# A gated delta rule on one core: the state of the recurrence in SBUF in place of PSUM

## The chip, the cores and the metric

The kernel runs on one core of a Trainium2 chip. The metric is the device time of one execution in microseconds; the median of three runs before the change is 888.05 us (886.9 to 889.43).

## The reference, cut to what matters

Two layers work on x of 16 x 512 x 128 (batch, tokens, width), in float32. The change touches the first layer's recurrence alone:

```python
# layer 0, attention: 16 heads of width 8; k = q = rmsnorm(x_act per head)
def step(S, inp):                     # S: [B, H, 8, 8], one matrix per batch and head
    q_t, k_t, v_t = inp
    S = S * lam
    err = v_t - jnp.einsum('bhk,bhkv->bhv', k_t, S)
    S = S + beta * (k_t[..., :, None] * err[..., None, :])
    o_t = jnp.einsum('bhk,bhkv->bhv', q_t, S)
    return (S, o_t)
_, o = jax.lax.scan(step, S0, (qT, kT, vT))        # 512 steps, one after the other

# layer 0, feed forward, beside it
h = silu(x @ w1.T * s1) * (x @ w2.T * s2)          # 128 -> 512
h = gelu(h @ h1.T * t1); h = gelu(h @ h2.T * t2)   # 512 -> 512, twice
y = h @ w3.T * s3                                  # 512 -> 128
```

A second layer with linear attention and a low-rank feed forward follows.

## The kernel before

The kernel has three stages, each with one instruction stream per engine: `prepare` (to about 179 us) makes keys, factors and right-hand sides for every batch; `recur_and_feed_forward` (about 179 to 617 us) runs the recurrence and the feed forward of the first layer side by side; `second_layer` does the rest.

In the second stage the recurrence lies on VectorE alone. The 256 pairs of batch and head are laid over 128 partitions in G = 2 groups. Four tokens are solved at once as a block (BLK = 4), so the 512 tokens are 128 blocks, one after the other. Each block is five VectorE instructions, each waiting for the one before:

- L910: the state (128 numbers a partition) times the four tokens' rows `tok_p`, written to `pg` (512 products a partition);
- L916: a sum over the 8 products and one more slot that ScalarE has filled with the right-hand side, written to `w`;
- L919: `w` times the block's keys `blk_k`, written to `kw` (512 a partition);
- L924: a sum over the four tokens, written to `gain` (128 a partition);
- L929: the new state, `lam4` x state + `gain`, in one SCALAR_TENSOR_TENSOR with a per-partition scalar.

Four blocks are a phase (PH = 4), 32 phases in all. Two PSUM banks `rec[0]` and `rec[1]` alternate by phase. Each holds `w` of a phase in its first 256 columns and, before the change, the state in the next 128. `pg`, `tok_p`, `blk_k`, `kw` and `gain` are in SBUF. The trace calls what lies in these banks `r_rec`.

The feed forward of the 16 batches runs on the other engines. TensorE multiplies (L1133 to L1140; L1165 to L1170 for the output). ScalarE applies the activations and splits each operand into an upper part (L1048, L1053). GpSimd (POOL) multiplies the two gates (`gate`, L943) and subtracts the upper parts to get the lower ones (`rest`, L935), for `f_gl`, `f_hl` and `f_xl`; it lays the tokens and keys of a segment too (L958, L966). All of POOL's operands in this stage are in SBUF. POOL's order is written out in its `batch`.

The two halves are tied in three places. ScalarE's `serve(n, i)` stands at four points of every batch and, where a phase is due, waits for `s_ok` (the state after the phase's last block), saves `w` (`save_w`, L1014) and fills the right-hand sides of the phase after next (`lay_r`, L1003). VectorE waits for `w_saved` before the last L929 of a phase, and for `r_laid` before the first L916. After the last phase ScalarE saves `w`, SyncE stores it (L846), and only when these stores have landed does the block of the stage end and `second_layer` begin.

Of the kernel before, what the change touches and what calls it, by code (L numbers as in the profile page):

```python
# [12 lines left out]
H, DH = 16, 8  # L13
HID = 512
P = 128
# [17 lines left out]
def build(nc, io, out):  # L33

    scr = {}
    for name in ("xnT", "P", "K", "R", "fac", "W"):
        scr[name] = nc.dram_tensor("scratch_" + name, [B, P, L], F32).ap()
    scr["xf"] = nc.dram_tensor("scratch_xf", [B, L, D], F32).ap()
    with ExitStack() as ctx:
        c = constants(nc, ctx)  # L40
        prepare(nc, io, scr, c)
        recur_and_feed_forward(nc, io, scr, c)
        second_layer(nc, io, scr, c, out)
# [703 lines left out]
def recur_and_feed_forward(nc, io, scr, c):  # L747
# [11 lines left out]
    TPH = PH * BLK  # L759
    SEGPH = BSEG // PH  # L760
    NPH = NSEG * SEGPH
    VG = DH * G
# [3 lines left out]
    with ctx:  # L766
        def sb(name, shape, dt=F32):
            return ctx.enter_context(nc.sbuf_tensor(name, shape, dt))
# [4 lines left out]
        def bank(name, shape):  # L773
            return ctx.enter_context(nc.psum_tensor(name, shape, F32))
# [10 lines left out]

        rec = [bank(f"r_rec{q}", [P, L]) for q in range(2)]
        w_of = [r[:, 0:VG * TPH].rearrange("p (a t) -> p a t", t=TPH) for r in rec]
        state = [r[:, VG * TPH:VG * TPH + VG * DH] for r in rec]

        x_f = c.first_x  # L790
        x_h, x_l = sb("f_xh", [P, L], F32R), sb("f_xl", [P, L], F32R)
# [866 lines left out]
```

## Time and profile before

| | before |
|---|---|
| median of 3 runs | 888.05 us |
| profiled execution, its own time | 888.89 us |
| its span, first to last instruction | 887.2 us |
| busy TensorE / VectorE / ScalarE / POOL, share of the span | 85% / 84% / 66% / 69% |
| mean granted TensorE clock | 0.943 |

A row of the trace gives the line in the kernel, the engine, the operation, the tiles written and read, their shapes and how often; then times. DVE is VectorE, ACT is ScalarE, PE is TensorE, SPq is SyncE's queue. What stands behind "<-" in brackets is what an idle engine had waited for, as the profile infers it.

### The profile page before, as it was taken

The numbers are of one execution on the slowest core, as the hardware profiler recorded it, in microseconds if no ns is written. First come the engines' busy times: TensorE is split into PE (matmuls) and PEld (weight loads), VectorE is DVE, ScalarE is ACT, GpSimd is POOL, SyncE is SP. The second block draws the span as 40 slices with busy tenths as digits, with TensorE's granted clock in tenths as the row PEclk, the third lists the DMA queues.
The fourth block names the chain that finished last, engine by engine and source line by source line (L and its number), as shares of the span: only waits on it lengthen the run. The fifth ranks groups of instructions, "written<-read, shape, count | busy, mean of one in ns | idle before, by whom it ended". The sixth has DMA issues, their size and how long they took to land. (4 is left out here: it accounts for less than half of the span.)

```text
span 887.2 us, 12736 instructions
## 1 busy us (share of the span) xinstructions
PE 751.5 (85%) x3422; PEld 531.0 (60%) x3422; DVE 747.8 (84%) x1424; ACT 584.7 (66%) x1319; POOL 608.2 (69%) x556
## 2 busy tenths in 40 slices
PE   1678888368999999999999999970389999999997
PEld 1444343146777778877777778860246666666664
DVE  2677888789999999999899898997268899989885
ACT  3666788267868777787787877720566667666631
POOL 1356888568776678686877666700298898989872
PEclk9998999759999999999999999995589999999998
DMA  6245665440511515125061160110411313222000
GB/s 172 75 164 171 222 226 206 170 96 1 106 37 35 131 35 113 53 57 109 0 130 35 35 130 24 48 36 24 143 37 48 96 52 93 61 84 84 24 25 25
DMA packets 135200, 75.68 MB, mean 85 GB/s; under 512 B 73962, under 2 KB 117612, under 8 KB 135148
## 3 DMA queue, kind: packets, MB, share of 16 engines
q1 hardware_dynamic: 132892, 72.22, 29.0%
q10 hardware_dynamic: 2256, 2.88, 1.0%
q8 instruction: 18, 0.29, 0.2%
q14 instruction: 34, 0.28, 0.1%
HBM read 41.53 MB, written 33.55 MB: 85 GB/s over the span
## 5 line engine op out<-in xcount | busy, mean ns | idle before, releaser
L935 POOL TENSOR_TENSOR f_hl<-f_h,f_hh 128x512 fp32r<-128x512 f32 x64 | 82.5, 1293 | 88.4 <-ACT f_hh L1053 88.3
L1347 POOL TENSOR_TENSOR l_kv<-l_qkv 128x1024 f32<-128x1024 f32 x64 | 124.8, 1950 | 24.7 <-PE l_ps_s L1568 21.7
L1133 PE MATMUL f_ps<-f_gh,w_hi 128*128 128x512 f32 x256 | 104.5, 408 | 6.8 <-POOL f_gl L935 6.8
L916 DVE TENSOR_REDUCE r_rec<-r_pg 128x64 f32<-128x576 f32 x128 | 97.4, 761 | 7.2
L1133 PE MATMUL f_ps<-f_hh,w_hi 128*128 128x512 f32 x256 | 102.5, 400 | 0.4 <-ACT f_b L1042 0.4
L1486 DVE TENSOR_TENSOR l_qs<-l_ps_s,l_qd 128x1024 f32<-128x1024 f32 x64 | 78.3, 1224 | 23.0 <-issue 11.2
L910 DVE TENSOR_TENSOR r_pg<-r_rec,r_pt 128x512 f32<-128x512 f32 x128 | 88.6, 692 | 6.3 <-POOL r_pt L958 1.1
L943 POOL TENSOR_TENSOR f_g<-f_a,f_b 128x512 f32<-128x512 f32 x64 | 81.6, 1286 | 16.3 <-ACT f_b L1042 16.3
L919 DVE TENSOR_TENSOR r_kw<-r_rec,r_kb 128x512 f32<-128x512 f32 x128 | 88.5, 691 | 4.4
L924 DVE TENSOR_REDUCE r_gain<-r_kw 128x128 f32<-128x512 f32 x128 | 87.8, 686 | 4.4
L935 POOL TENSOR_TENSOR f_gl<-f_g,f_gh 128x512 fp32r<-128x512 f32 x64 | 82.0, 1292 | 3.2 <-ACT f_gh L1048 3.2
L1492 DVE TENSOR_REDUCE l_o_in<-l_qs 128x128 f32<-128x1024 f32 x64 | 77.5, 1211 | 0.6
L1135 PE MATMUL f_ps<-f_gl,w_hi 128*128 128x512 f32 x192 | 77.6, 404 | 0.0
L1135 PE MATMUL f_ps<-f_hl,w_hi 128*128 128x512 f32 x192 | 75.7, 394 | 0.0
L1048 ACT ACTIVATE f_gh<-f_g 128x512 fp32r<-128x512 f32 x64 | 41.1, 642 | 52.1 <-POOL f_g L943 51.6
L1133 PE MATMUL f_ps<-f_xh,w_hi 128*128 128x512 f32 x128 | 54.9, 429 | 22.4 <-ACT f_a L1038 13.6
L1567 PE MATMUL l_ps_s<-l_kv,tri 128*128 128x512 f32 x128 | 66.9, 604 | 2.9 <-DVE l_qs L1486 2.9
L1170 PE MATMUL f_ps<-w,f_e 128*128 128x128 f32 x512 | 67.6, 275 | 0.0
L1568 PE MATMUL l_ps_s<-l_kv,tri 128*128 128x512 f32 x128 | 65.4, 593 | 0.0
L1052 ACT ACTIVATE f_h<-f_ps,t 128x512 f32<-128x512 f32 x64 | 44.5, 695 | 31.0 <-PE f_ps L1140 30.8
L1417 ACT ACTIVATE l_qkv<-l_ps_q 128x384 f32<-128x384 f32 x64 | 31.3, 490 | 48.7 <-PE l_ps_q L1554 47.3
L1133 PEld LDWEIGHTS f_ps<-f_gh,w_hi 128*128 128x128 f32 x256 | 49.6, 194 | 22.2 <-POOL f_gl L935 8.2
(202 smaller groups left out, 1997.7 us busy)
## 6 DMA issues: line engine op xcount, KB each, us to landing
p_x<-in_L_attn_x_dram SPq DMA_DIRECT2D x16, 256.0 KB, 3.3
scratch_xnT<-p_xnT SPq DMA_DIRECT2D x16, 256.0 KB, 3.3
scratch_K<-p_kout SPq DMA_DIRECT2D x16, 256.0 KB, 3.4
scratch_fac<-p_fac SPq DMA_DIRECT2D x16, 256.0 KB, 3.5
scratch_R<-p_rr SPq DMA_DIRECT2D x16, 256.0 KB, 2.4
scratch_P<-p_pp SPq DMA_DIRECT2D x16, 256.0 KB, 2.0
first_x<-scratch_xnT SPq DMA_DIRECT2D x16, 256.0 KB, 2.8
first_xt<-in_L_attn_x_dram SPq DMA_DIRECT2D x16, 256.0 KB, 3.0
```

What stands on the lines that cost most here:

```text
L910: dve.tensor_tensor(pg[q][:, at, :, :, 0:DH].rearrange("p (v g) i k -> p v g i k", g=G), by_head(state[q]), of_tokens(tok_p[u], t), ALU.mu ...
L916: dve.tensor_reduce(w, pg[q][:, at, :, :, :], AX.X, ALU.add).then_inc(w_ok, 1)
L919: dve.tensor_tensor(kw[:, :, :].rearrange("p (v g k) i -> p v g k i", v=DH, g=G), w.rearrange("p (v g) i -> p v g i", g=G).unsqueeze(3).to ...
L924: dve.tensor_reduce(gain[:, :], kw[:, :, :], AX.X, ALU.add).then_inc(gain_ok, 1)
L935: pool.tensor_tensor(lower, full, upper.bitcast(F32), ALU.subtract).then_inc(done, 1)
L943: pool.tensor_tensor(g_f[:, j, :], a_f[:, j, :], b_f[:, j, :], ALU.mult).then_inc(gate_ok, 1)
L1133: nc.tensor.matmul(bank, c.w_hi[:, weights[k], :], upper[k], start=k == 0, stop=False)
L1135: nc.tensor.matmul(bank, c.w_hi[:, weights[k], :], lower[k], start=False, stop=False)
L1170: ins = nc.tensor.matmul(y_at[:, tokens], e_f[:, k, tokens], c.w3[:, k, :], start=False, stop=t == NT - 1 and k == NB - 1)
L1347: pool.tensor_tensor(dst, k, v, ALU.mult).then_inc(kv_ok, 1)
L1486: dve.tensor_tensor(qs[t % 2][:, :].rearrange("p (h v k) -> p h v k", h=H, k=DH), ps_s[:, :, :].rearrange("p a (h v k) -> p (a h) v k", h= ...
L1492: dve.tensor_reduce(out=o_in[n % 2][:, t, :].rearrange("p (h v) -> p h v", h=H), in_=qs[t % 2][:, :].rearrange("p (h v k) -> p h v k", h=H ...
```

## The change

The state gets two SBUF tensors of its own, of 128 numbers a partition each. Nothing else is edited: `w` stays in the two PSUM banks, and the five instructions, their order and their waits are the same. `state[q]` is read by L910 and L929 and written by L894 (the first zeros) and L929.

```diff
         rec = [bank(f"r_rec{q}", [P, L]) for q in range(2)]
         w_of = [r[:, 0:VG * TPH].rearrange("p (a t) -> p a t", t=TPH) for r in rec]
-        state = [r[:, VG * TPH:VG * TPH + VG * DH] for r in rec]
+        state = [sb(f"r_state{q}", [P, VG * DH])[:, :] for q in range(2)]
```

## Rows read from the trace of the kernel before

**Rows 1.** Busy time by window, the recurrence's stretch and its tail: window, length, engines, clock, DMA.
```profile
179.00:616.80 437.80, 391.43 (x1936) 317.51 (x1936) 408.20 (x640) 316.82 (x511) 291.25 (x236) 0.96 0.26 61
...
578.00:616.80 38.80, 14.94 (x96) 12.96 (x95) 36.55 (x58) 6.24 (x12) 0.50 (x1) 0.77 0.07 21
```

**Rows 2.** Timeline, end of the stage, ScalarE, SyncE, TensorE: start, length, instruction, idle before.
```profile
616.74 0.38 ACT L1014 ACTIVATE r_w<-r_rec 128x256 f32<-128x256 f32 x1 [13.15 <-DVE r_rec L929]
...
617.15 1.25 SPq L846 DMA_DIRECT2D scratch_W<-r_w  x2
...
592.71 1.06 PE L1170 MATMUL f_ps<-w,f_e 128*128 128x128 f32 x8
```

**Rows 3.** The lines that touch the state: duration ns min/median/max, first and last start.
```profile
L910 DVE TENSOR_TENSOR r_pg<-r_rec,r_pt x128: 690/692/694, 179.0 to 613.4; 128x512 f32<-128x512 f32 x128
...
L929 DVE SCALAR_TENSOR_TENSOR r_rec<-r_rec,lam,r_gain x128: 358/359/360, 182.1 to 616.3; 128x128 f32<-128x128 f32 x128
```

**Rows 4.** Timeline of VectorE over one block.
```profile
402.57 0.36 DVE L929 SCALAR_TENSOR_TENSOR r_rec<-r_rec,lam,r_gain 128x128 f32<-128x128 f32 x1
402.97 0.69 DVE L910 TENSOR_TENSOR r_pg<-r_rec,r_pt 128x512 f32<-128x512 f32 x1
...
405.94 0.36 DVE L929 SCALAR_TENSOR_TENSOR r_rec<-r_rec,lam,r_gain 128x128 f32<-128x128 f32 x1
```

**Rows 5.** VectorE groups that differ in where operands lie: busy us, mean ns or min/median/max.
```profile
L541 DVE SCALAR_TENSOR_TENSOR p_prod<-p_ps_k,cfac,p_kT 128x128 f32<-128x128 f32 x16 | 5.5, 342 | 0.0
...
L1498 DVE TENSOR_TENSOR l_past<-l_ps_kv,head_ones x48: 278/280/294, 649.0 to 875.7; 128x128 f32<-128x128 f32 x48
...
L1510 DVE TENSOR_TENSOR biases<-biases x1: 264/264/264, 623.5 to 623.5; 128x128 f32<-128x128 f32 x1
...
L531 DVE TENSOR_TENSOR p_keys<-p_xn,p_rrms x16: 678/692/1174, 24.8 to 155.6; 128x512 f32<-128x512 f32 x16
```

**Rows 6.** A short VectorE operation of two SBUF inputs, and POOL beside it.
```profile
L1460 DVE TENSOR_TENSOR l_nm<-l_mean,l_rs x16: 163/678/682, 634.4 to 840.5; 128x4 f32<-128x4 f32 x16
...
653.59 0.66 DVE L1460 TENSOR_TENSOR l_nm<-l_mean,l_rs 128x4 f32<-128x4 f32 x1
...
652.28 1.95 POOL L1347 TENSOR_TENSOR l_kv<-l_qkv 128x1024 f32<-128x1024 f32 x1 [0.79 <-PE l_ps_s L1568]
```

**Rows 7.** Timeline of VectorE and POOL around L531, the longest and one other.
```profile
155.64 1.17 DVE L531 TENSOR_TENSOR p_keys<-p_xn,p_rrms 128x512 f32<-128x512 f32 x1
...
155.23 1.04 POOL L346 TENSOR_TENSOR p_kout<-p_kT,kfac 128x512 f32<-128x512 f32 x1
...
111.05 0.68 DVE L531 TENSOR_TENSOR p_keys<-p_xn,p_rrms 128x512 f32<-128x512 f32 x1
...
111.42 1.16 POOL L256 TENSOR_TENSOR p_tmp_p<-p_coup,p_pp 128x384 f32<-128x384 f32 x1 [0.32 <-ACT p_coup L439]
...
37.40 1.00 POOL L256 TENSOR_TENSOR p_tmp_p<-p_coup,p_pp 128x384 f32<-128x384 f32 x1 [6.78 <-ACT p_coup L439]
```

**Rows 8.** POOL's costliest groups in the recurrence's stretch: busy us, mean ns, idle before.
```profile
L935 POOL TENSOR_TENSOR f_hl<-f_h,f_hh 128x512 fp32r<-128x512 f32 x64 | 82.5, 1293 | 88.4 <-ACT f_hh L1053 88.3
L935 POOL TENSOR_TENSOR f_gl<-f_g,f_gh 128x512 fp32r<-128x512 f32 x64 | 82.0, 1292 | 3.2 <-ACT f_gh L1048 3.2
L943 POOL TENSOR_TENSOR f_g<-f_a,f_b 128x512 f32<-128x512 f32 x64 | 81.6, 1286 | 16.3 <-ACT f_b L1042 16.3
```

**Rows 9.** Timeline of POOL: two operations back to back, and one spaced by ScalarE.
```profile
414.44 2.55 POOL L935 TENSOR_TENSOR f_gl<-f_g,f_gh 128x512 fp32r<-128x512 f32 x2
...
424.82 1.29 POOL L935 TENSOR_TENSOR f_hl<-f_h,f_hh 128x512 fp32r<-128x512 f32 x1 [0.59 <-ACT f_hh L1053]
```

**Rows 10.** TensorE after an idle stretch, twice, and the window behind the first.
```profile
218.78 0.50 PE L1133 MATMUL f_ps<-f_gh,w_hi 128*128 128x512 f32 x1 [1.74 <-POOL f_gl L935]
...
219.80:223.20 3.40, 3.18 (x8) 2.56 (x9) 3.14 (x6) 3.39 (x8) 1.41 (x2) 0.50 0.27 67
...
256.54 0.50 PE L1133 MATMUL f_ps<-f_xh,w_hi 128*128 128x512 f32 x1 [1.44 <-ACT f_a L1038]
```

## The prediction, made before the changed kernel was run

> **What bounds the kernel now.** I read the busy time by window first, because the change lies in one stage. From 179.0 to 616.8 us VectorE runs 640 instructions, the 128 blocks of five, and is busy 408.20 of 437.80 us; TensorE is busy 391.43 us, POOL 291.25 us with 236 operations [rows 1]. Both TensorE and VectorE look like the bound there. The end of the stage decides. The timeline of ScalarE shows it idle for 13.15 us before its last save of `w`, for L929, and SyncE's store of `w` follows at 617.15 us [rows 2]; from 578 us on POOL has one operation (of 236) and VectorE is busy 36.55 of 38.80 us [rows 1]. So the feed forward is over well before the recurrence, and the second layer waits for the recurrence. TensorE's last matmuls of the stage end at 593.8 us [rows 2]: the feed forward has 23 us of room. Every nanosecond added to each block is 128 ns on the end.
>
> Next the blocks. L910 takes 690 to 694 ns and L929 358 to 360 ns over all 128 [rows 3]. Nothing disturbs them, though POOL is at work two thirds of the time. One block lasts 405.94 - 402.57 = 3.37 us from L929 to L929; L910 starts 0.04 us after the end of L929 (402.93 to 402.97), and from the end of L910 (403.66) to the next L929 are 2.28 us, filled by L916, L919 and L924 [rows 4].
>
> **What is removed and added, 1: the operations themselves.** No instruction comes or goes. L910 gets its first input from SBUF in place of PSUM; its nearest row of the same shape with both inputs in SBUF, L531, has the median 692 ns, the same as L910 now [rows 3, 5]: nothing gained. L929 gets its state from SBUF and writes it there. The nearest rows: the same operation with a PSUM input but an SBUF output and a per-partition scalar, L541, 342 ns against 359 ns; and TENSOR_TENSOR of 128 columns with one PSUM input, 280 ns (L1498), against 264 ns with none (L1510) [rows 3, 5]. So L929 gains 17 ns for its output and 0 to 16 ns for its input. I take 17 ns, since the reading of the input shows 0 in L910's pair: 128 x 0.017 = 2.2 us gained, at most 128 x 0.033 = 4.2 us. The zeroing of the state (L894) is one instruction and moves by nothing that counts.
>
> The Trainium skill would price this part otherwise. Its page "VectorE: DVE Perf Modes", in the table under "The TRN2 errata", gives VectorE a fixed 58 cycles from SBUF against 120 from PSUM at 0.96 GHz. By it each of the 256 instructions would gain 62 cycles, 65 ns, together an estimated 16.5 us. The pairs of rows above show 0 and 16 ns for it.
>
> **2: what the two instructions now have in common with POOL.** After the change L910 reads two SBUF inputs (state and `tok_p`), and L929 too (state and `gain`). Before it each had one in PSUM. The trace has operations of that kind beside POOL. L1460 (two SBUF inputs, 4 columns) takes 163 ns at its shortest but 678 ns as the median of 16 [rows 6]. At 653.59 us it starts while POOL's L1347 runs (652.28 to 654.23) and ends at 654.25: it takes its 0.16 us only as POOL ends [rows 6]. The remainder of POOL's operation was 0.64 us and the delay 0.66 - 0.16 = 0.50 us, so the delay is the remainder less 0.14. L531 shows the same at 155.64 us: 1.174 us in place of 0.692, a delay of 0.48 us against a remainder of 0.63 us [rows 5, 7]. It goes the other way too: POOL's L256 starts at 111.42 us in L531 and takes 1.16 us, where it takes 1.00 us alone; the remainder of L531 was 0.31 us [rows 7]. So the two exclude each other, whoever is there first keeps the other out, and the second starts about 0.14 us before the first's recorded end.
>
> The Trainium skill, "SBUF — State Buffer", "Who interferes with whom", has this as a rule: a VectorE instruction with two SBUF inputs contends with a GpSimd instruction that reads SBUF for a shared port, and the first holds it for its whole length. It speaks against this change, and by it alone, with holds of the whole 1.29 us, the same working as below would give an estimated 0.39 us in place of 0.31 for each operation, 978 us in place of 959. Rows 6 and 7 bear out who waits, but show the hold 0.14 us shorter, and I go by them.
>
> **The price.** POOL has 236 operations in the stretch [rows 1], of which 192 take 82.5 + 82.0 + 81.6 us, 1.28 to 1.29 us each [rows 8], and the other 44 the rest, some 1.0 us each; I price all as the 192, which asks at most 4 us too much. Take one of 1.29 us that comes at a random time of a block of 3.36 us.
> - If it is running when L929 starts, L929 waits 0 to 1.29 - 0.14 = 1.15 us, 0.57 us in the mean. The chance is 1.15 / 3.36 = 0.34, the share 0.195 us.
> - If it comes in the 0.36 us of L929 or the 0.04 us behind it, it runs before L910 gets its turn. L910 then waits from 0.97 us (POOL held back until 0.14 us before L929's end: 1.29 - 0.14 - 0.04 = 1.11 left, less 0.14) to 1.15 us (POOL just begun), about 1.0 us. The chance is 0.40 / 3.36 = 0.12, the share 0.12 us.
> - If it comes in L910 it waits itself, at most 0.55 us, and then runs under L916 and L919, which read `w` or `pg` and have at most one SBUF input that matters: no delay.
>
> Together 0.31 us for each operation of POOL, 236 x 0.31 = 73 us.
>
> A second reading of the same trace, without chance: of the 128 starts of L929, 74 fall into a running operation of POOL, and the remainders less 0.14 us sum to 40.0 us; 29 operations of POOL start in L929 or within 0.40 us of its start, at about 1.0 us each 29 us. That is 69 us (the 128 starts run from 182.1 to 616.3 us [rows 3], POOL's 236 operations stand in the same window [rows 1]).
>
> A third for the densest stretches, where POOL starts every 1.25 us [rows 9]: after L910 two of its operations fit into 2.28 us plus 0.14 and L929 is hardly late; the third comes in L929, and L910 waits 0.97 us for it. That is about 0.95 us for three operations, 0.32 us each. Where POOL is spaced by 1.86 us [rows 9] against blocks of 3.36 us there is no fixed relation, and the first sum holds.
>
> I take 73 us. Less 2.2 us it is 71 us on the recurrence, whose stretch becomes 437.8 + 71 = 509 us.
>
> **What stands beside it.** The feed forward is held up too: operations of POOL that come in L910 or L929 wait up to 0.55 or 0.22 us. 40 of them start in L910 and 29 in or near L929; at 0.28 and 0.1 us that is 14 us if all lay on its path, less than its 23 us of room and far less than 23 + 71. So it costs nothing. It will rather be held back: ScalarE waits at `serve` once a phase, some 71 / 32 = 2 us each. TensorE then idles. After an idle stretch of 1.74 us the granted clock fell from 1.0 to 0.50 (the lower of TensorE's two levels, 1.2 GHz against 2.4) for 3.4 us, and after one of 1.44 us matmuls kept 0.50 us and less, the pace of the full clock [rows 10]. A fall per phase would cost 1.7 us of TensorE's work each, 32 x 1.7 = 54 us, under the 94 us of room that it then has. Costed at nothing, too. Nothing in stages one and three reads the state.
>
> **The sum** against the profiled execution: 888.89 + 73 - 2.2 = 959.7 us. The median of the runs was 0.84 us lower, so I forecast 959 us.
>
> **The rivals.**
> - *No contention* (faster). The recurrence's two instructions would be left alone because their records now are, and only their operands' place counts: 2.2 to 4.2 us gained, 884 to 886 us; by the skill's table 872 us, worked out above. For it: L541 and L1498, 48 times within 278 to 294 ns [rows 5], are undisturbed beside POOL. Against it: both have a PSUM input, and L1460 was held in 14 of 16. It decides if a two-input instruction with a broadcast input doesn't take part; L531 has one and was held. 0.05 for faster; 0.03 that the gain and a handful of collisions cancel.
> - *POOL yields* (slower by little). If VectorE always came first, POOL would pay: 128 x (0.55 + 0.22) = 99 us of its time is closed, two thirds of it in use, some 65 us; beyond the 23 us of room the feed forward would end the stage 42 us later, 928 us. Against it: rows 6 show VectorE as the one that waits. 0.04.
> - *POOL first at every hand-over* (slower). In the dense stretches a third operation of POOL takes its turn before L929, and a fourth before L910: 1.24 + 0.97 us for four operations, 0.56 us each. For all 236 that is 132 us, 1018 us. It asks that the next operation's request counts from the end of the one before, though it starts behind L929's. 0.07.
> - *The clock* (slower). If TensorE falls to 1.2 GHz for 10 us rather than 3.4 at every pause, it loses 5 us a phase, 160 us in all, and the feed forward sets the end: 888.9 - 23 + 160 = up to 1025 us. Against it: such a feed forward would leave no pauses, and the clock would stay up; the two meet near 975 to 990 us. 0.08.
>
> **How the numbers follow.** The forecast case has 0.73, with its own range 930 to 990: the price per operation between 0.19 us (only L929's share counts: 236 x 0.195 - 2 = 44 us, 932 us) and 0.44 us (half-way to POOL first: 104 - 2 = 102 us, 990 us). Outside lie the faster and same cases (0.08), part of POOL first and of the clock; I reach up to 1000 for the clock and down to 926 for POOL yields. The range is 926 to 1000 us. Faster by over 0.3% 0.05, within 0.3% 0.03, slower by over 0.3% 0.92; 0.3% is about what a measurement of this kernel can tell from no change.
>
> **What would show each step.** Durations of L910 and L929 now constant would spread: L910's median near 692 ns with a tail to about 1.8 us, L929's minimum 340 to 345 ns with a tail to 1.5 us; their sum would grow by some 71 us, while L916, L919 and L924 keep their 2.28 us from the end of L910 to the start of L929 [rows 4]. Each long one ends 0.02 to 0.1 us from the end of a POOL operation. The stretch of the recurrence ends near 688 us, ScalarE waits for L929 once a phase, TensorE's share of the stage falls from 0.89 to 0.77, and the second layer is unchanged. The prediction is wrong if L910 and L929 stay constant, or if ScalarE no longer waits for L929 at the end.

## The result and the profile after

The changed kernel takes 973.07 us as the median of four runs, the kernel before 888.24 us in the same comparison: 1.0953 times as long, with a 95% interval of 1.0928 to 1.0978. The forecast was 959 us, with 926 to 1000 us as its range. The profiled execution took 974.93 us with a span of 973.2 us, 86.0 us more than the span before.

The first view is part 5 of the page of the changed kernel, the five lines of the recurrence (line, engine, operation, shapes and count, then busy us, mean ns, and idle us before them):

```profile
L910 DVE TENSOR_TENSOR r_pg<-r_state,r_pt 128x512 f32<-128x512 f32 x128 | 143.2, 1119 | 6.2 <-POOL r_pt L958 1.1
...
L916 DVE TENSOR_REDUCE r_rec<-r_pg 128x64 f32<-128x576 f32 x128 | 97.4, 761 | 7.2
L919 DVE TENSOR_TENSOR r_kw<-r_rec,r_kb 128x512 f32<-128x512 f32 x128 | 88.5, 691 | 4.5
L924 DVE TENSOR_REDUCE r_gain<-r_kw 128x128 f32<-128x512 f32 x128 | 87.8, 686 | 4.4
...
L929 DVE SCALAR_TENSOR_TENSOR r_state<-r_state,lam,r_gain 128x128 f32<-128x128 f32 x128 | 81.0, 632 | 4.6
```

L910 has grown from 88.6 us (128 x 692 ns, [rows 3]) to 143.2 us and L929 from 46.0 us to 81.0 us. The other three keep their mean lengths of the trace before (761, 691 and 686 ns). The idle time before L929 was 8.3 us in the same part of the page before and is 4.6 us now. 54.6 + 35.0 - 3.7 = 85.9 us: that is the whole difference.

The same two lines in the view of single lines (ns min/median/max) answer to [rows 3], where both were flat:

```profile
L910 DVE TENSOR_TENSOR r_pg<-r_state,r_pt x128: 691/694/1805, 179.0 to 699.4; 128x512 f32<-128x512 f32 x128
...
L929 DVE SCALAR_TENSOR_TENSOR r_state<-r_state,lam,r_gain x128: 350/352/1510, 182.1 to 702.4; 128x128 f32<-128x128 f32 x128
```

More than half of the instances are undisturbed, the others are up to 1.16 us longer. Counted over all 128: 58 of L910 are longer by 54.8 us in all over their undisturbed length, 53 of L929 by 35.9 us. The timeline shows against what. First VectorE, then POOL, in a dense stretch of gate products:

```profile
423.30 1.47 DVE L929 SCALAR_TENSOR_TENSOR r_state<-r_state,lam,r_gain 128x128 f32<-128x128 f32 x1
424.80 1.64 DVE L910 TENSOR_TENSOR r_pg<-r_state,r_pt 128x512 f32<-128x512 f32 x1
...
428.72 0.35 DVE L929 SCALAR_TENSOR_TENSOR r_state<-r_state,lam,r_gain 128x128 f32<-128x128 f32 x1
429.10 1.67 DVE L910 TENSOR_TENSOR r_pg<-r_state,r_pt 128x512 f32<-128x512 f32 x1
...
433.05 0.35 DVE L929 SCALAR_TENSOR_TENSOR r_state<-r_state,lam,r_gain 128x128 f32<-128x128 f32 x1
```

```profile
423.34 1.27 POOL L935 TENSOR_TENSOR f_gl<-f_g,f_gh 128x512 fp32r<-128x512 f32 x1
424.57 1.31 POOL L943 TENSOR_TENSOR f_g<-f_a,f_b 128x512 f32<-128x512 f32 x1
425.85 2.99 POOL L935 TENSOR_TENSOR f_gl<-f_g,f_gh 128x512 fp32r<-128x512 f32 x2
428.81 1.41 POOL L935 TENSOR_TENSOR f_xl<-first_x,f_xh 128x512 fp32r<-128x512 f32 x1
```

L929 starts at 423.30 and POOL's L935 0.04 us later, and yet L929 is the one that waits: it ends at 424.77, so its own 0.35 us began at 424.42, 0.19 us before POOL's recorded end (424.61). POOL's next operation has started at 424.57, inside L929, and now L910 waits for it: it ends at 426.44, so its 0.69 us began at 425.75, 0.13 us before that operation's end (425.88). The two POOL operations from 425.85 take 2.99 us in place of some 2.55, because the first came in L910 and is held back itself. At 428.72 L929 is free, since POOL comes 0.09 us behind it, and L910 is held. This last block, 428.72 to 433.05, lasts 4.33 us, the one before it 5.42.

It is the same for all 111 held instances: the work of the 53 of L929 begins 0.20 to 0.21 us before the end of a POOL operation that reads SBUF, that of the 58 of L910 0.13 to 0.15 us. Near ties at L929 mostly go to POOL: in 11 of the 53 the POOL operation started after L929, by up to 0.08 us, and only twice did L929 stay free of an operation that came as close behind it. At L910 there was no such tie to see.

The end of the stage, SyncE, ScalarE and TensorE, answers to [rows 2]:

```profile
702.74 0.38 ACT L1014 ACTIVATE r_w<-r_rec 128x256 f32<-128x256 f32 x1 [13.13 <-DVE r_state L929]
703.14 1.25 SPq L846 DMA_DIRECT2D scratch_W<-r_w  x2
...
669.83 1.06 PE L1170 MATMUL f_ps<-w,f_e 128*128 128x128 f32 x8
```

The recurrence still sets the end, 86.0 us later than before, and the feed forward ends 31.8 us ahead of it.

### The profile page after: what moved, and what is told of

It is laid out like the page before. It is cut to its first block and busy times, and to the rows that moved or that the text cites. A ratio compares the mean times of both kernels' runs of the same rounds, so it can differ in the third digit from the quotient of the medians.

```text
span 973.2 us, 12736 instructions
## 1 busy us (share of the span) xinstructions
PE 783.4 (81%) x3422; PEld 550.8 (57%) x3422; DVE 838.0 (86%) x1424; ACT 582.7 (60%) x1319; POOL 635.9 (65%) x556
## 5 line engine op out<-in xcount | busy, mean ns | idle before, releaser
L935 POOL TENSOR_TENSOR f_hl<-f_h,f_hh 128x512 fp32r<-128x512 f32 x64 | 87.0, 1379 | 114.0 <-ACT f_hh L1053 113.9
L910 DVE TENSOR_TENSOR r_pg<-r_state,r_pt 128x512 f32<-128x512 f32 x128 | 143.2, 1119 | 6.2 <-POOL r_pt L958 1.1
L1133 PE MATMUL f_ps<-f_xh,w_hi 128*128 128x512 f32 x128 | 63.5, 496 | 58.0 <-ACT f_a L1038 37.1
L943 POOL TENSOR_TENSOR f_g<-f_a,f_b 128x512 f32<-128x512 f32 x64 | 89.1, 1401 | 31.9 <-ACT f_b L1042 31.9
L916 DVE TENSOR_REDUCE r_rec<-r_pg 128x64 f32<-128x576 f32 x128 | 97.4, 761 | 7.2
L935 POOL TENSOR_TENSOR f_gl<-f_g,f_gh 128x512 fp32r<-128x512 f32 x64 | 90.7, 1427 | 11.4 <-ACT f_gh L1048 11.4
L919 DVE TENSOR_TENSOR r_kw<-r_rec,r_kb 128x512 f32<-128x512 f32 x128 | 88.5, 691 | 4.5
L924 DVE TENSOR_REDUCE r_gain<-r_kw 128x128 f32<-128x512 f32 x128 | 87.8, 686 | 4.4
L1014 ACT ACTIVATE r_w<-r_rec 128x256 f32<-128x256 f32 x32 | 12.4, 386 | 128.6 <-DVE r_state L929 128.6
L929 DVE SCALAR_TENSOR_TENSOR r_state<-r_state,lam,r_gain 128x128 f32<-128x128 f32 x128 | 81.0, 632 | 4.6
L1170 PE MATMUL f_ps<-w,f_e 128*128 128x128 f32 x512 | 75.4, 296 | 0.0
L1133 PEld LDWEIGHTS f_ps<-f_xh,w_hi 128*128 128x128 f32 x128 | 28.0, 219 | 79.6 <-ACT f_a L1038 44.3
L1170 PEld LDWEIGHTS f_ps<-w,f_e 128*128 128x128 f32 x512 | 70.8, 214 | 0.0
L1567 PE MATMUL l_ps_s<-l_kv,tri 128*128 128x512 f32 x128 | 66.9, 604 | 2.9 <-DVE l_qs L1486 2.9
```

The source lines that it names most:

```text
L910: dve.tensor_tensor(pg[q][:, at, :, :, 0:DH].rearrange("p (v g) i k -> p v g i k", g=G), by_head(state[q]), of_tokens(tok_p[u], t), ALU.mu ...
L916: dve.tensor_reduce(w, pg[q][:, at, :, :, :], AX.X, ALU.add).then_inc(w_ok, 1)
L919: dve.tensor_tensor(kw[:, :, :].rearrange("p (v g k) i -> p v g k i", v=DH, g=G), w.rearrange("p (v g) i -> p v g i", g=G).unsqueeze(3).to ...
L924: dve.tensor_reduce(gain[:, :], kw[:, :, :], AX.X, ALU.add).then_inc(gain_ok, 1)
L935: pool.tensor_tensor(lower, full, upper.bitcast(F32), ALU.subtract).then_inc(done, 1)
L943: pool.tensor_tensor(g_f[:, j, :], a_f[:, j, :], b_f[:, j, :], ALU.mult).then_inc(gate_ok, 1)
```

## The experiments

All are edits of the changed kernel but for the second. The comparisons stand against runs of the kernel before on the same chip, whose medians were 889.7 to 890.2 us. "Excess" is the sum, over the 128 instances in the profiled execution, of what each took beyond its undisturbed length, and a held instance is one that took over 40 ns more.

**The gain in PSUM, so that L910 alone has two SBUF inputs.**

```diff
-        gain = sb("r_gain", [P, VG * DH])
...
+        gain_at = [r[:, VG * TPH:VG * TPH + VG * DH] for r in rec]
...
-                            dve.tensor_reduce(gain[:, :], kw[:, :, :], AX.X, ALU.add).then_inc(gain_ok, 1)
+                            dve.tensor_reduce(gain_at[q], kw[:, :, :], AX.X, ALU.add).then_inc(gain_ok, 1)
...
-                            dve.scalar_tensor_tensor(out=state[after], in0=state[q], scalar=c.lam4[:, :], in1=gain[:, :],
+                            dve.scalar_tensor_tensor(out=state[after], in0=state[q], scalar=c.lam4[:, :], in1=gain_at[q],
```

> The state stays in SBUF and the block's gain goes to the PSUM columns that the state has left, so L929 has one SBUF input (state) and one PSUM input (gain), and L910 alone still has two SBUF inputs. Theory (two SBUF inputs exclude POOL): L929 is constant near 350 to 360 ns as before, L910 alone is held, in some 60 to 75 of 128 blocks and by about 0.6 us in the mean (it now meets POOL operations at a random point), 236 x 0.195 = 46 us, so the time is about 932 us (920 to 945). Rival (an instruction that reads the state from SBUF is slowed by POOL's traffic whatever its other input is): L929 is still stretched by some 36 us, and the time stays near 973 us.

It took 937.74 us, 1.0525 times the kernel before (1.0498 to 1.0552). The view of single lines:

```profile
L910 DVE TENSOR_TENSOR r_pg<-r_state,r_pt x128: 691/1067/1816, 181.3 to 665.2; 128x512 f32<-128x512 f32 x128
...
L929 DVE SCALAR_TENSOR_TENSOR r_state<-r_state,lam,r_rec x128: 346/348/350, 184.4 to 668.1; 128x128 f32<-128x128 f32 x128
```

L929 reads the same state from the same SBUF tensor beside the same POOL operations and is flat in all 128; what differs is that its second input is in PSUM. So it is not the reading of SBUF that is held but the pair. L910 is held 77 times, excess 53.5 us, where I expected 46.

The trace shows where the 7 us more come from: POOL's operations are no random arrivals here either. VectorE, then POOL, in a stretch of gate products:

```profile
409.90 1.52 DVE L910 TENSOR_TENSOR r_pg<-r_state,r_pt 128x512 f32<-128x512 f32 x1
...
414.09 1.53 DVE L910 TENSOR_TENSOR r_pg<-r_state,r_pt 128x512 f32<-128x512 f32 x1
```

```profile
410.83 1.73 POOL L943 TENSOR_TENSOR f_g<-f_a,f_b 128x512 f32<-128x512 f32 x1
412.53 2.54 POOL L935 TENSOR_TENSOR f_gl<-f_g,f_gh 128x512 fp32r<-128x512 f32 x2
```

POOL's operation of 410.83 us comes in the first L910, waits, and runs as L910 ends. The two behind it follow without a gap, and the second of them is still running (to 415.07) when the next L910 starts at 414.09: it is 0.84 us longer. Of the 77 holds 34 are of 0.74 to 0.86 us and make 27.6 of the 53.5 us; spread evenly over 0 to 1.15 us, some 8 of the 77 would lie there.

**L929 alone with two SBUF inputs.** The kernel before, state in PSUM, with a constant tensor of zeros in the state's place in L929, so the old state is left out of the update.

```diff
+        still = sb("r_still", [P, VG * DH])
...
+                dve.memset(still[:, :], 0.0)
...
-                            dve.scalar_tensor_tensor(out=state[after], in0=state[q], scalar=c.lam4[:, :], in1=gain[:, :],
+                            dve.scalar_tensor_tensor(out=state[after], in0=still[:, :], scalar=c.lam4[:, :], in1=gain[:, :],
```

> The kernel before (state in PSUM), but L929 takes its first input from a constant SBUF tensor of zeros in place of the state, so the old state is left out of the update; its output goes to PSUM. L929 has two SBUF inputs, L910 has not. Theory: L910 stays at 692 ns in all blocks, L929 is held in about 74 blocks and by 40 to 46 us in all, time about 931 us (920 to 942). Together with the run with the gain in PSUM the two parts then sum to about the whole 85 us, if held L929 and held L910 don't make each other likelier; if a held L929 draws the next POOL operation in front of L910 (43 of 53 times in the changed kernel), each part alone is a different mixture: L910 hits that follow a held L929 are missing here. Rival (the SBUF read or write of the state is what costs, not the pair): L929 undisturbed, 888 us.

It took 923.73 us, 1.0363 times (1.0334 to 1.0393). The lines (L912 and L931 are L910 and L929 here):

```profile
L912 DVE TENSOR_TENSOR r_pg<-r_rec,r_pt x128: 691/691/695, 180.1 to 648.5; 128x512 f32<-128x512 f32 x128
...
L931 DVE SCALAR_TENSOR_TENSOR r_rec<-r_still,lam,r_gain x128: 359/719/1477, 183.2 to 651.5; 128x128 f32<-128x128 f32 x128
```

The other way round: L910 is flat, L929 held 76 times with an excess of 38.2 us. The count of the trace before had said 74 times and 40.0 us. Both parts alone sum to 53.5 + 38.2 = 91.7 us, the change to 54.8 + 35.9 = 90.7 us. That the sums agree doesn't show that the two add up: in the changed kernel most of L910's excess stands behind a held L929 (below), and where L910 is held alone there is none.

**POOL writes but does not read.** In the 208 gate products and lower parts:

```diff
-                    pool.tensor_tensor(lower, full, upper.bitcast(F32), ALU.subtract).then_inc(done, 1)
+                    pool.memset(lower.bitcast(F32), 0.0).then_inc(done, 1)
...
-                    pool.tensor_tensor(g_f[:, j, :], a_f[:, j, :], b_f[:, j, :], ALU.mult).then_inc(gate_ok, 1)
+                    pool.memset(g_f[:, j, :], 0.0).then_inc(gate_ok, 1)
```

> The changed kernel, but POOL's gate products and lower parts (L935, L943, 208 operations) are memsets of the same tiles: they write SBUF and read none, and the feed forward's values are left out. The 28 copies of tokens and keys stay. Theory (only operations of POOL that read SBUF and VectorE's with two SBUF inputs exclude each other): L910 and L929 are held by the 28 copies alone, 28 x 0.385 = 11 us, the recurrence's stretch is about 445 us and the time about 895 us (886 to 905). Rival (writes count as well): memsets hold it too, in proportion to their length; at 0.5 us and more each that is some 20 to 40 us more, 915 us or above.

It took 893.29 us, 1.0035 times (1.0021 to 1.0048). The excess is 9.1 us, 5 instances of L929 and 7 of L910, and each of the 12 lies over one of the 28 copies. Of the instances that are not held 89 overlap a memset by more than 0.1 us. The timeline shows both, VectorE and POOL:

```profile
201.88 1.12 DVE L929 SCALAR_TENSOR_TENSOR r_state<-r_state,lam,r_gain 128x128 f32<-128x128 f32 x1
203.04 1.46 DVE L910 TENSOR_TENSOR r_pg<-r_state,r_pt 128x512 f32<-128x512 f32 x1
...
201.78 2.17 POOL L966 COPY r_kb<-r_k 128x512 f32<-128x512 f32 x2
...
407.95 0.69 DVE L910 TENSOR_TENSOR r_pg<-r_state,r_pt 128x512 f32<-128x512 f32 x1
...
407.82 0.53 POOL L943 MEMSET f_g<- 128x512 f32 x1
```

The copies (201.78 to 203.95) hold L929 and then L910; the memset (407.82 to 408.35) runs through L910's first half and it takes its 0.69 us. So POOL's reads are what excludes, and its writes don't. The Trainium skill, "SBUF — State Buffer", "Who interferes with whom", says just this of two SBUF inputs against a GpSimd instruction that only writes, and the run agrees: 0 of 89 held.

**The same bytes in twice as many instructions.** Each gate product and each lower part is cut into two of 256 columns:

```diff
-                    pool.tensor_tensor(lower, full, upper.bitcast(F32), ALU.subtract).then_inc(done, 1)
+                    for half in (slice(0, L // 2), slice(L // 2, L)):
+                        ins = pool.tensor_tensor(lower[:, half], full[:, half], upper[:, half].bitcast(F32), ALU.subtract)
+                    ins.then_inc(done, 1)
... (the same for the gate products)
```

> The changed kernel, with each gate product and each lower part of POOL cut into two instructions of 256 columns, the same bytes in twice as many instructions of an estimated 0.73 us. Theory (who comes first keeps the other out for its whole instruction): a wait is at most as long as one instruction, so L910 and L929 are held more often but for less: (0.59 x 0.59 / 2 + 0.40 x 0.43) / 3.36 = 0.10 us for each of 416, with the copies about 52 us, with follow-ups some 60 us; time about 945 us (930 to 957), longest L910 about 1.3 us in place of 1.8. Rival (the two share a bandwidth, and what costs is POOL's traffic): nothing changes but POOL's own length, 973 us or slower.

It took 944.48 us, 1.0609 times (1.0581 to 1.0638):

```profile
L910 DVE TENSOR_TENSOR r_pg<-r_state,r_pt x128: 691/1101/1460, 179.2 to 668.0; 128x512 f32<-128x512 f32 x128
...
L929 DVE SCALAR_TENSOR_TENSOR r_state<-r_state,lam,r_gain x128: 352/532/1224, 182.3 to 671.0; 128x128 f32<-128x128 f32 x128
```

More are held (81 and 88), each for less (longest L910 1.46 us in place of 1.81), excess 59.6 us. A shared bandwidth would have left it at 90.7 us, since the bytes are the same and POOL is busier (361.6 us in the recurrence's stretch against 318.9). The wait is for one instruction, and shorter instructions make shorter waits.

**w in SBUF too**, a third instruction of the block with two SBUF inputs:

```diff
-        w_of = [r[:, 0:VG * TPH].rearrange("p (a t) -> p a t", t=TPH) for r in rec]
+        w_of = [sb(f"r_solved{q}", [P, VG * TPH])[:, :].rearrange("p (a t) -> p a t", t=TPH) for q in range(2)]
```

> The changed kernel with w in SBUF as well, so that no tensor of the recurrence is in PSUM. L919 (w times keys) then has two SBUF inputs too, a third instruction of the block. Theory: L919 is held where POOL runs at its start, another 0.195 us for each of 236 operations less what no longer falls on L929, +25 to +46 us on the changed kernel: about 1008 us (995 to 1022). Rival (POOL's operations are bound to meet L910 or L929 in any case, so a third meeting point adds nothing): 973 us.

It took 986.13 us, 1.1067 times (1.1015 to 1.1119), 13 us more than the changed kernel: between the two expectations, nearer to the rival's.

```profile
L910 DVE TENSOR_TENSOR r_pg<-r_state,r_pt x128: 691/1448/1777, 183.6 to 714.6; 128x512 f32<-128x512 f32 x128
...
L919 DVE TENSOR_TENSOR r_kw<-r_solved,r_kb x128: 691/792/1832, 185.3 to 716.1; 128x512 f32<-128x512 f32 x128
...
L929 DVE SCALAR_TENSOR_TENSOR r_state<-r_state,lam,r_gain x128: 351/526/1278, 186.8 to 717.6; 128x128 f32<-128x128 f32 x128
```

L919, flat everywhere else, is now held 69 times, which confirms the rule for a third line. But its excess is 16.5 us, L929's has fallen from 35.9 to 18.5 us and L910's has risen from 54.8 to 67.8: in all 102.8 us against 90.7 (this profiled execution, of 990.09 us, was the longest of its four). My price per line and operation, 0.195 us, does not add up over more lines. That a meeting with POOL is mostly moved from one line to another, and seldom added, is how I read it; no run shows it by itself.

**What doubled L910's share.** In the changed kernel a held L929 is followed by a held L910 in 43 of 53 cases, and only 15 of L910's 58 stand alone. The 43 make 39.9 us of L910's excess, the 15 make 14.7 us. The trace shows why this can be: POOL's next operation is queued right behind the one that held L929 (424.57 above) and comes in L929. If so, anything that keeps POOL's next reading operation away for 0.25 us should free L910. Here a useless write stands behind each gate product and each lower part:

```diff
+        filler = sb("f_filler", [P, 384])
...
+                def fill():
+                    if fills:
+                        pool.wait_ge(filled, len(fills))
+                    fills.append(pool.memset(filler[:, :], 0.0).then_inc(filled, 1))
...
                     pool.tensor_tensor(lower, full, upper.bitcast(F32), ALU.subtract).then_inc(done, 1)
+                    fill()
... (and behind the gate products)
```

> The changed kernel, and behind each gate product and each lower part POOL writes zeros to a tile of 384 columns that nobody reads (a memset, some 0.4 us, no SBUF input). POOL's next reading operation then starts 0.4 us or more after the one before it has ended, later than the 0.25 us after which a held L929 is followed by L910. Theory (L910's excess is twice what I had forecast because POOL's next operation, queued right behind the one that held L929, comes in L929 and runs before L910): blocks in which both are held fall from 43 to under 10, L929's excess stays at 30 to 40 us, L910's falls from 54.7 to 20 to 30 us, time 945 to 955 us, though POOL has 208 instructions more. Rival (L910 is held as often as it is because POOL is busy, whatever stands before): L910's excess stays at 50 us or more, and the time at 973 us or above.

It took 934.08 us, 1.0504 times (1.0477 to 1.053): 39 us less than the changed kernel, with 208 more instructions on POOL. The lines (L912 and L931 are L910 and L929 here), and, from the groups by line, what POOL adds:

```profile
L912 DVE TENSOR_TENSOR r_pg<-r_state,r_pt x128: 691/692/1658, 181.9 to 660.2; 128x512 f32<-128x512 f32 x128
...
L931 DVE SCALAR_TENSOR_TENSOR r_state<-r_state,lam,r_gain x128: 351/604/1426, 185.0 to 663.2; 128x128 f32<-128x128 f32 x128
...
L941 POOL MEMSET f_filler<- 128x384 f32 x208 | 86.7, 417 | 0.0
```

Held L929 that are followed by a held L910 fall from 43 to 6, L910's excess from 54.8 to 8.2 us. L929's stays at 35.5 us, though spread over 103 instances in place of 53. So the follow-up is shown: it goes when POOL's next read comes later. Less is left than I had expected (8.2 in place of 20 to 30 us), and that is not the follow-up alone, which made 39.9 of the 54.8 us: of the 15 held L910 that stood alone 4 are left too. The writes set the distance of all of POOL's reads, behind a held L929 or not, and this run doesn't part the two effects.

**Fewer reading operations.** Only the 64 lower parts of the hidden layers become memsets, so they are left out of the products:

```diff
-                    rest(h_f[:, o, :], h_h[:, o, :], h_l[:, o, :], hl_ok)
+                    pool.memset(h_l[:, o, :].bitcast(F32), 0.0).then_inc(hl_ok, 1)
```

> The changed kernel with only the 64 lower parts of the hidden layers (f_hl) replaced by memsets, so that 172 reading operations of POOL remain in the stretch, and those lower parts are left out of the products. Theory (a price for each reading operation): the excess of L910 and L929 together is between the 9.1 us of 28 operations and the 90.7 us of 236, near 172 x 0.385 = 66 us; the time about 949 us (940 to 957). Rival (the dense runs of the gates cost it, and the spaced f_hl little): the excess stays above 80 us, the time above 962 us.

It took 955.55 us, 1.0735 times (1.071 to 1.076), with an excess of 69.9 us (29.5 on L929, 40.4 on L910). With 28, 172 and 236 reading operations the excess is 9.1, 69.9 and 90.7 us, 0.33, 0.41 and 0.38 us each: nearly in proportion. The dense gates cost a little more than the spaced `f_hl`.

None of these beats the kernel before.

## Why the prediction was right, and which term was off

- **The bound.** That the recurrence alone sets the stage's end, and that each nanosecond of a block counts 128 times, held: 85.9 us more on VectorE, 86.0 us more in the span.
- **The exclusion.** Read from L1460 and L531 [rows 6, 7], it was right in its kind, in who waits and in its length of one instruction. The 0.14 us that it takes off the remainder hold for L910 (0.13 to 0.15); for L929 they are 0.20 us. The runs with one of the two inputs back in PSUM, with POOL writing only and with POOL's operations halved each show a part of it.
- **L929's share.** Forecast 0.195 x 236 = 46 us, or 40 us by the count over the trace; measured 35.9 us, and 38.2 us alone. The count over the rows was the better reading, since POOL's operations are no random arrivals.
- **L910's share** is the term that was mis-sized: forecast 0.12 x 236 = 28 us (29 us by the count), measured 54.8 us. The step that was off is the one that let POOL's operations come at a random time into the 0.40 us of L929. Behind a held L929 POOL's next operation is queued and came there in 43 of 53 cases, for 39.9 of the 54.8 us. The third working, for dense stretches, had a steady state in which L929 is free and L910 waits 0.97 us. It occurs (the block from 428.72 to 433.05), but it hangs on a margin of under 0.1 us: POOL's third operation comes 0.08 us behind L929 in that working, and up to 0.08 us behind it still goes first. Then both wait, as in the block from 423.30. So the rival "POOL first at every hand-over" had a part in it, 11 of L929's 53, at some 1.1 us each 12 us; as a rule for all 236, with its 0.56 us each, it was too much. With L929 10 us under and L910 27 us over the forecast the two together came to 90.7 us in place of 73, 0.385 us an operation in place of 0.31. The forecast of the time is so near in part by luck: the one miss hides 10 of the other's 27 us.
- **L929 itself.** Forecast 17 ns gained, measured 359 - 352 = 7 ns where it is not held, 0.9 us in all. With the first input moved to SBUF and the output left in PSUM it is still 359 ns, so what is gained is the output's place, and nothing the first input's. That agrees with the pair L910 and L531 [rows 3, 5]. It doesn't agree with the 65 ns that the table of the Trainium skill, "VectorE: DVE Perf Modes", "The TRN2 errata", would have given.
- **A gain not seen.** VectorE's three waits for `w_saved` before L929 (at 437.4, 492.4 and 535.1 us), 3.7 us, are gone. The likely reason is that the slower recurrence no longer runs ahead of ScalarE. I had not counted them. The misses sum to the whole: 17.7 us more of holding, 1.3 us less gained on L929, 3.7 us fewer waits, so 15.3 us; the profiled execution took 974.93 us against the sum's 959.7.
- **The feed forward** cost nothing, as forecast. TensorE was expected at a share of 0.77 of the stage and is at 421.73 of 523.8 us, 0.81. It is busy 30 us longer [rows 1], as its granted clock in the stage fell from 0.96 to 0.88:

```profile
178.50:702.30 523.80, 421.73 (x1936) 336.66 (x1936) 497.56 (x639) 314.65 (x511) 318.89 (x237) 0.88 0.23 51
...
441.00:446.50 5.50, 2.71 (x11) 1.53 (x9) 5.29 (x7) 1.77 (x4) 3.89 (x3) 1.00 0.00 0
446.60:456.70 10.10, 5.16 (x19) 4.73 (x20) 9.30 (x14) 7.99 (x13) 4.56 (x4) 0.50 0.87 154
```

In the second window TensorE is busy 2.71 of 5.50 us at the full clock; in the third, behind it, the clock is at the lower level for 10 us. ScalarE waited for L929 128.6 us in 25 pieces, where it had waited 22.9 us in 3, so the room was there, and the rival of the clock did not decide. Its lengths of up to 10 us were seen, its effect on the end was not.
- **The signs.** Two that I had named came out otherwise. A long L929 does not end 0.02 to 0.1 us from the end of a POOL operation but 0.15 us behind it, and a long L910 0.55 us behind it; for L910 the forecast's own 0.14 us had said as much (0.69 - 0.14). And L929's shortest is 350 ns, not 340 to 345.

## What to carry to other kernels

Before an operand of a VectorE instruction is moved from PSUM to SBUF, look whether the other tensor input is in SBUF too and whether POOL works beside it. If both, look in the trace for a short VectorE operation of that kind that is longer than it should be, and take POOL's remainder at its start as the price; count over the real rows rather than with a chance, and follow POOL's queue on from there, since the next operation gets in between two dependent VectorE instructions. One PSUM input on such an instruction kept it free in every run here (all 128 of L910 or L929), at 7 to 9 ns where an output goes to PSUM for it. Where it can't be had, short POOL instructions (excess 59.6 in place of 90.7 us), or writes between its reads (43.7 us), cut the waits.

## What the hardware showed that I had not expected

- 208 added POOL instructions of 417 ns made the kernel 39 us faster (973.07 to 934.08 us), by where they keep the next read.
- The place of the first input made no difference (L929 359 ns with it in PSUM or in SBUF), and with the second in PSUM L929 was 4 ns shorter (348 against 352 ns). Writing PSUM costs VectorE 7 to 9 ns an instruction: L929 359 against 352 ns, and the two lines below, L924 with its output in PSUM in the first experiment (686 ns in SBUF) and L916 with its output in SBUF in the run with `w` there (761 ns in PSUM).

```profile
L924 DVE TENSOR_REDUCE r_rec<-r_kw x128: 694/695/697, 183.7 to 667.4; 128x128 f32<-128x512 f32 x128
```

```profile
L916 DVE TENSOR_REDUCE r_solved<-r_pg x128: 752/753/755, 184.5 to 715.3; 128x64 f32<-128x576 f32 x128
```

Two things stay open: how much of the 39 us that the added writes gave back is the follow-up and how much the wider spacing of the reads, and why near ties at L929 went to POOL in 11 cases and not in 2.
